# Graph attention on one core: digit products for two pairs at a time, and two PSUM banks for Q's products

## The chip, the cores and the metric

The kernel runs on one core of a Trainium2 chip. The metric is the device time of one execution in microseconds; lower is better.

## The reference

One layer of graph attention on 6,250 nodes with 512 features (8 heads of 64) and 106,250 edges, sorted by their target node `dst`, then two normalisations:

```python
Q, K, V = x @ Wq, x @ Wk, x @ Wv                    # each (6250, 8, 64)
score = einsum('ehd,ehd->eh', K[src], Q[dst]) / 8
score = exp(clip(score, -5, 5))
wV = segment_sum(V[src] * score[..., None], dst)    # (6250, 8, 64)
Z = segment_sum(score, dst)
h = x + wV / (Z + 1e-6)
h = (h - mean_over_nodes(h)) * rsqrt(var + 1e-5) * gamma + beta
out = layernorm(x + h)
```

## The kernel before

There are three stages, one behind the other. `project` computes Q, K and V by node and writes them to HBM, and builds the tables of the edges. `attend` walks over the edges. `normalise` does the rest. The change is in `attend` alone.

`attend` cuts the edges into visits of 128, each of which belongs to one tile of 128 target nodes. Two visits make a pair; there are 440 pairs. A ring has 8 places (`RING`), so the place `s` of pair `q` is `q % 8`. For a pair the engines do this:

- POOL gathers the 1024 K and V values of each edge's source node from HBM (L498), 6 pairs ahead of its own weighing.
- TensorE makes, from 7 binary digits of the target node within its tile, products that are equal to 7 where edge and node agree (`mm_ps`: L649 for the two visits by edge, L651 for both by node). These are called the digit products.
- ScalarE turns them into one-hot matrices by Relu with a bias of -7 (`mm_sb`, L582).
- TensorE multiplies the one-hots by the tile's Q, held as a high and a low part: four products of 512 columns, which bring Q's rows to the edges (`q_ps`, L640).
- VectorE multiplies them into K (L536), sums by head (L543) and clips (L546).
- ScalarE takes Exp (L585) and weighs 4 of V's 8 heads (L573, eight instructions a pair). VectorE weighs 2 heads (one pair later) and POOL 2 heads (six pairs later), both at L465.
- TensorE adds the weighed rows to their nodes in `acc` through the one-hots (L662). Where a tile ends, ScalarE copies it to `agg` (L567) and sets its bank to zero (L569): an eviction, 49 in all.

Each engine runs its own list of steps, one for each pair `q`, in an order written out by hand. Semaphores tie them together:

- ScalarE's step q: the Relu of pair q+3; then the wait for the clip, Exp and, in even steps, a DMA issue for the digits `lb`; the eight weighings of q; an eviction behind pair q-3, if one is due.
- TensorE's step q: Q's products of pair q+1; the digit products of q+3, which wait for the Relu of q+2 since there is one bank `mm_ps`; the products into `acc` for q-2.
- VectorE's step q: the multiply of q, the weighing of q-1, the reduction and the clip of q.

`q_ps` has three banks. A pair uses two of them, the middle one every time, in turn with the first and the last. The visit whose bank is free goes first; the other waits for VectorE's multiply of the pair before (`s_mul`).

Of the kernel before, what the change touches and what calls it, by code (L numbers as in the profile page):

```python
# [384 lines left out]
def attend(nc, kv_d, q_d, lb_d, nb_d, tabs, agg, soft):  # L385
    src_t, bits_row, cnt_row, ident = tabs
    with ExitStack() as ctx:
        def sb(name, shape, dt):
            return ctx.enter_context(nc.sbuf_tensor(name, shape, dt))
# [10 lines left out]
        kv = sb("kv", [P, RING, 2, KVW], F32)  # L400
        idx = sb("idx", [P, RING, 2], I32)
        q_tile = sb("q_tile", [P, 2, 2 * DIM], F32)
        mm_sb = sb("mm_sb", [P, RING, 4 * P], F32R)
        lb = sb("lb", [P, RING, 2 * P], BF16)
        nb = sb("nb", [P, P], BF16)
        raw = sb("raw", [P, RING, 2, HEADS], F32)
# [1 line left out]
        idle = sb("idle", [P, 1], F32)  # L408
        less = sb("less", [P, 1], F32)
        acc = ps("acc", [P, 2, 2 * DIM], F32)  # L410
        mm_ps = ps("mm_ps", [P, 4 * P], F32)
        q_ps = ps("q_ps", [P, 3, DIM], F32)


        s_g = [soft[f"s_g{s}"] for s in range(RING)]
        s_mul, s_red, s_clip, s_exp = sems("s_mul"), sems("s_red"), sems("s_clip"), sems("s_exp")
        s_t, s_mm, s_v, s_seg = sems("s_t"), sems("s_mm"), sems("s_v"), sems("s_seg")
        s_lb = [sem(f"s_lb{g}") for g in range(RING // LB_PAIRS)]
        s_idx = [sem(f"s_idx{g}") for g in range(RING // IDX_PAIRS)]
        s_nb, s_zero, s_qx, s_q, s_evc, s_evict = (sem("s_nb"), sem("s_zero"), sem("s_qx"), sem("s_q"),  # L420
# [20 lines left out]
        def follow(eng, tiles):  # L441
            now, before = eng.alloc_register("mask_now"), eng.alloc_register("mask_before")
            regs = [eng.alloc_register(f"tile_{n}") for n in range(tiles)]
            for r in (now, *regs):
                eng.reg_mov(r, 0)

            def fetch(mask):
                eng.reg_mov(before, now)
                if not isinstance(mask, int) or mask < MASKS:
                    eng.reg_load(now, bits_row[0:1, bass.ds(mask, 1)])  # L450

            def bit(k, earlier=False):
                mask = eng.snap(before if earlier else now, min_val=0, max_val=2 ** VBODY - 1)
                return (mask >> k) & 1
            fetch(0)
            return regs, fetch, bit

        def heads(ap):
            return ap.rearrange("p a (h d) -> p a h d", d=D_HEAD)
# [7 lines left out]
        with nc.Block() as block:  # L467
# [55 lines left out]
            @block.vector  # L523
            def _(dve):
                dve.memset(less[:, :], -float(BITS))
                dve.memset(lb[:, :, :], 0.0)
                dve.memset(nb[:, :], 0.0)
                dve.memset(zeros[:, :], 0.0).then_inc(s_zero, 1)

                def step(q, s, fills):  # L530
                    s1, f1 = at(s, fills, -1)
                    if there(q):
                        dve.wait_ge(s_g[s], 32 * fills)
                        dve.wait_ge(s_qx, q + 1)
                        k = kv[:, s, :, 0:DIM]
                        dve.tensor_tensor(k, q_ps[:, s % 2:s % 2 + 2, :], k,  # L536
                                          ALU.mult).then_inc(s_mul[s], 1)
                    if there(q - 1):
                        dve.wait_ge(s_exp[s1], f1)
                        weigh(dve, s1, ACT_HEADS, HEADS - ACT_HEADS - POOL_HEADS).then_inc(s_v[s1], 1)  # L540
                    if there(q):
                        dve.wait_ge(s_mul[s], fills)
                        dve.tensor_reduce(raw[:, s, :, :], heads(kv[:, s, :, 0:DIM]), AX.X,  # L543
                                          ALU.add).then_inc(s_red[s], 1)
                        dve.wait_ge(s_red[s], fills)
                        dve.tensor_scalar(raw[:, s, :, :], raw[:, s, :, :], -5.0, 5.0, ALU.max,  # L546
                                          ALU.min).then_inc(s_clip[s], 1)

                pipeline(dve, step)

            @block.scalar
            def _(act):
# [20 lines left out]
                    return act.activation(v, v, ACT.Copy, scale=kv[:, s, u, 2 * DIM + h:2 * DIM + h + 1])  # L573

                def step(q, s, fills):
                    e, a = q - LAG, q + 3
                    se, fe = at(s, fills, -LAG)
                    sa, fa = at(s, fills, 3)
                    if there(a):
                        act.wait_ge(s_t[sa], fa)  # L580
                        wait(act, s_seg[sa], fa - 1)
                        act.activation(mm_sb[:, sa, :], mm_ps[:, :], ACT.Relu, bias=less[:, 0:1]).then_inc(s_mm[sa], 1)  # L582
                    if there(q):
                        act.wait_ge(s_clip[s], fills)
                        act.activation(kv[:, s, :, 2 * DIM:KVW], raw[:, s, :, :], ACT.Exp).then_inc(s_exp[s], 1)  # L585
                        act.wait_ge(s_exp[s], fills)
                    if not isinstance(q, int) or q >= 0 and there(q + RING):
                        if s % LB_PAIRS == 0:
                            bits_of(q + RING, s)
                    if there(q):  # L590
                        for u in range(2):
                            for h in range(ACT_HEADS):
                                last = weighed(s, u, h)
                        last.then_inc(s_v[s], 1)
                    if there(e):
                        t0 = act.snap(tile_reg, min_val=0, max_val=TILES - 1)
                        over = act.snap(sum(bit((2 * (s - LAG) + n + VBODY - 2) % VBODY,
                                                earlier=2 * (s - LAG) + n + VBODY - 2 < VBODY) for n in (1, 2)),
                                        min_val=0, max_val=2)
                        with act.If(over > 0):  # L600
                            act.wait_ge(s_seg[se], fe)
                            evict(t0)
                            with act.If(over > 1):
                                evict((t0 + 1).with_bounds(min_val=1, max_val=TILES - 1))
                        act.reg_mov(tile_reg, t0 + over)
                    if s == RING - 1:
                        fetch(q // RING + 2 if isinstance(q, int) else fills + 1)
# [3 lines left out]
            def _(pe):  # L611
# [10 lines left out]
                def step(q, s, fills):  # L622
                    a, b, c = q + 3, q + 1, q - 2
                    (sa, fa), (sb_, fb), (sc, fc) = at(s, fills, 3), at(s, fills, 1), at(s, fills, -2)
                    if there(b):
                        tiles = []
                        for u in range(2):
                            v = 2 * sb_ + u
                            tile = pe.snap(pe.snap(tile_regs[(v - 1) % PLACES], min_val=0, max_val=TILES - 1)
                                           + bit(2 * s + u), min_val=0, max_val=TILES - 1)  # L630
                            pe.reg_mov(tile_regs[v % PLACES], tile)
                            tiles.append(tile)
                        pe.wait_ge(s_mm[sb_], fb)
                        pe.wait_ge(s_q, 16 * (tiles[1] + 1))
                        for u in ((0, 1), (1, 0))[sb_ % 2]:
                            if u == 1 - sb_ % 2:
                                wait(pe, s_mul[s], fills)
                            for n in range(2):
                                part_q = q_tile[:, bass.ds(tiles[u] % 2, 1), n * DIM:(n + 1) * DIM].bitcast(F32R)
                                last = pe.matmul(q_ps[:, sb_ % 2 + u, :], mm_sb[:, sb_, (2 + u) * P:(3 + u) * P],  # L640
                                                 part_q, start=(n == 0), stop=(n == 1))
                        last.then_inc(s_qx, 1)
                    if there(a):
                        if sa % LB_PAIRS == 0:
                            pe.wait_ge(s_lb[sa // LB_PAIRS], 16 * fa)
                        m1, f1 = at(s, fills, 2)
                        wait(pe, s_mm[m1], f1)
                        for u in range(2):
                            pe.matmul(mm_ps[:, u * P:(u + 1) * P], lb[:, sa, u * P:(u + 1) * P], nb[:, :],  # L649
                                      start=True, stop=True)  # L650
                        pe.matmul(mm_ps[:, 2 * P:4 * P], nb[:, :], lb[:, sa, :], start=True,  # L651
                                  stop=True).then_inc(s_t[sa], 1)
                    if there(c):
                        tiles = [pe.snap(tile_regs[(2 * sc + u) % PLACES], min_val=0, max_val=TILES - 1)
                                 for u in range(2)]
# [1 line left out]
                        pe.wait_ge(s_evict, tiles[1] + 1)  # L657
                        for u in range(2):
                            par = tiles[u] % 2
                            m = mm_sb[:, sc, u * P:(u + 1) * P].bitcast(F32)  # L660
                            for n in range(2):
                                last = pe.matmul(acc[:, bass.ds(par, 1), DIM - (1 - n) * HALF:DIM + n * HALF], m,  # L662
                                                 kv[:, sc, u, DIM + n * HALF:DIM + (n + 1) * HALF],
                                                 start=False, stop=True, skip_group_check=True)
# [299 lines left out]
```

## Time and profile before

| | |
|---|---|
| median of 3 runs | 2182.51 us (2182.19 to 2183.84) |
| the profiled execution | 2179.65 us, of which its span is 2177.7 |
| TensorE, VectorE, ScalarE, POOL busy | 95%, 74%, 66%, 62% of the span |
| edge stage, first to last multiply of VectorE | 530.4 to 1978.7 us |
| granted TensorE clock, mean | 0.989 of 2.4 GHz |

Times are microseconds from the span's start, unless they are marked ns. PE is TensorE's multiplication and PEld its weight load; DVE is VectorE, ACT ScalarE, POOL GpSimd. An idle time is put down to what ended it; "issue" is time in which the engine waited for nothing that the profile shows. Instructions of an engine overlap a little, so that sums of durations exceed busy time.

### The profile page before, as it was taken

The numbers are of one execution on the slowest core, as the hardware profiler recorded it, in microseconds if no ns is written. First come the engines' busy times: TensorE is split into PE (matmuls) and PEld (weight loads), VectorE is DVE, ScalarE is ACT, GpSimd is POOL, SyncE is SP. The second block draws the span as 40 slices with busy tenths as digits, with TensorE's granted clock in tenths as the row PEclk, the third lists the DMA queues.
The fourth block names the chain that finished last, engine by engine and source line by source line (L and its number), as shares of the span: only waits on it lengthen the run. The fifth ranks groups of instructions, "written<-read, shape, count | busy, mean of one in ns | idle before, by whom it ended". The sixth has DMA issues, their size and how long they took to land. (4 is left out here: it accounts for less than half of the span.)

```text
span 2177.7 us, 42941 instructions
## 1 busy us (share of the span) xinstructions
PE 2075.5 (95%) x8167; PEld 1328.3 (61%) x8168; DVE 1610.7 (74%) x2268; ACT 1429.6 (66%) x4869; POOL 1347.1 (62%) x1612
## 2 busy tenths in 40 slices
PE   8999999996999999999999999999999999998998
PEld 3444444443677677777777677777777777775343
DVE  3115311112899999999999999999899999998968
ACT  0001000101788888888888888888888888888745
POOL 2001444443788888888888888888888888882000
PEclk9999999998999999999999999999999999999999
DMA  5334665675799999899999899999899999996224
GB/s 182 132 120 155 229 220 214 224 238 214 269 322 325 319 328 321 313 321 323 318 331 325 311 318 325 318 332 323 308 322 323 317 329 330 312 315 217 89 97 174
DMA packets 184590, 588.14 MB, mean 270 GB/s; under 512 B 29072, under 2 KB 30832, under 8 KB 184560
## 3 DMA queue, kind: packets, MB, share of 16 engines
q0 software_dynamic: 135904, 465.14, 60.8%
q1 hardware_dynamic: 38080, 95.18, 12.5%
q10 hardware_dynamic: 10576, 27.50, 3.3%
q8 instruction: 9, 0.15, 0.0%
q14 instruction: 21, 0.17, 0.0%
HBM read 534.48 MB, written 78.91 MB: 282 GB/s over the span
## 5 line engine op out<-in xcount | busy, mean ns | idle before, releaser
L498 POOL DMA_INDIRECT kv<-kv_d,idx x880 | 905.1, 1029 | 236.1 <-issue 231.5
L573 ACT ACTIVATE kv<-kv 128x64 f32<-128x64 f32 x3520 | 889.2, 335 | 131.3 <-issue 76.5
L662 PE MATMUL acc<-kv,mm_sb 128*128 128x260 f32 x3520 | 875.8, 392 | 37.7 <-POOL kv L465 19.1
L662 PEld LDWEIGHTS acc<-kv,mm_sb 128*128 128x128 f32 x3520 | 635.4, 190 | 175.7 <-issue 96.2
L640 PE MATMUL q_ps<-q_tile,mm_sb 128*128 x1760 | 580.1, 445 | 23.1 <-issue 18.0
L536 DVE TENSOR_TENSOR kv<-q_ps,kv 128x1024 f32<-128x1024 f32 x440 | 538.4, 1224 | 48.5 <-PE q_ps L640 28.7
L543 DVE TENSOR_REDUCE raw<-kv 128x16 f32<-128x1024 f32 x440 | 532.3, 1210 | 0.0
L640 PEld LDWEIGHTS q_ps<-q_tile,mm_sb 128*128 128x128 f32 x1760 | 326.1, 189 | 130.1 <-issue 77.6
L270 ACT COPY kv_sb<-kv_ps 128x1024 f32<-128x1024 f32 x49 | 49.6, 1012 | 464.7 <-PE kv_ps L247 464.7
L247 PE MATMUL kv_ps<-w_sb,x_sb 128*128 128x512 f32 x784 | 344.5, 592 | 0.0
L582 ACT ACTIVATE mm_sb<-mm_ps,less 128x512 fp32r<-128x512 f32 x440 | 296.7, 674 | 68.0 <-PE mm_ps L651 41.7
L312 DVE TENSOR_SCALAR q_sb<-q_ps 128x512 fp32r<-128x512 f32 x49 | 33.9, 692 | 387.0 <-PE kv_ps L247 387.0
L465 POOL TENSOR_TENSOR kv<-kv 128x256 f32<-128x256 f32 x440 | 281.4, 640 | 17.5 <-ACT kv L585 9.3
L465 DVE TENSOR_TENSOR kv<-kv 128x256 f32<-128x256 f32 x440 | 235.2, 535 | 57.2 <-ACT kv L585 31.1
L247 PEld LDWEIGHTS kv_ps<-w_sb,x_sb 128*128 128x128 f32 x784 | 148.9, 190 | 187.5 <-issue 187.0
L247 PE MATMUL q_ps<-w_sb,x_sb 128*128 128x512 f32 x392 | 179.0, 599 | 6.9 <-DMA w_sb<-in_wq 6.9
L247 PEld LDWEIGHTS q_ps<-w_sb,x_sb 128*128 128x128 f32 x392 | 75.1, 192 | 101.3 <-issue 92.7
L649 PE MATMUL mm_ps<-nb,lb 128*128 128x128 bf16 x880 | 126.3, 225 | 5.4 <-ACT mm_sb L582 4.8
L546 DVE TENSOR_SCALAR raw<-raw 128x16 f32<-128x16 f32 x440 | 117.7, 267 | 15.2
L649 PEld LDWEIGHTS mm_ps<-nb,lb 128*128 128x128 bf16 x880 | 50.9, 98 | 125.7 <-issue 120.6
L651 PE MATMUL mm_ps<-lb,nb 128*128 128x256 bf16 x440 | 120.8, 275 | 0.0
L213 POOL DMA_DIRECT2D xb<-in_x x49 | 26.3, 536 | 131.4 <-DMA xb_d<-xb 128.6
(113 smaller groups left out, 971.4 us busy)
## 6 DMA issues: line engine op xcount, KB each, us to landing
kv_d<-kv_sb ACTq DMA_DIRECT2D x49, 512.0 KB, 4.4
q_d<-q_sb SPq DMA_DIRECT2D x49, 512.0 KB, 4.5
q_tile<-q_d SPq DMA_DIRECT2D x49, 512.0 KB
x_res<-xb_d SPq DMA_DIRECT2D x56, 256.0 KB, 5.3
kv<-kv_d,idx POOLq DMA_INDIRECT x880
x_sb<-in_xT SPq DMA_DIRECT2D x49, 256.0 KB, 2.7
xb<-in_x POOLq DMA_DIRECT2D x49, 256.0 KB, 3.0
xb_d<-xb POOLq DMA_DIRECT2D x49, 256.0 KB, 2.9
```

The lines of the kernel that those rows point to most:

```text
L247: last = pe.matmul(out, x_sb[j][:, c, :], w_sb[:, n, c, :], start=(c == 0), stop=(c == CHUNKS - 1))
L465: return eng.tensor_tensor(v, v, w, ALU.mult)
L498: pool.indirect_dma_start(kv[:, s, u, 0:2 * DIM], None, kv_d, bass.IndirectOffsetOnAxis(idx[:, s, u:u + 1], 0), bounds_check=N_NODES - 1, ...
L536: dve.tensor_tensor(k, q_ps[:, s % 2:s % 2 + 2, :], k, ALU.mult).then_inc(s_mul[s], 1)
L543: dve.tensor_reduce(raw[:, s, :, :], heads(kv[:, s, :, 0:DIM]), AX.X, ALU.add).then_inc(s_red[s], 1)
L546: dve.tensor_scalar(raw[:, s, :, :], raw[:, s, :, :], -5.0, 5.0, ALU.max, ALU.min).then_inc(s_clip[s], 1)
L573: return act.activation(v, v, ACT.Copy, scale=kv[:, s, u, 2 * DIM + h:2 * DIM + h + 1])
L582: act.activation(mm_sb[:, sa, :], mm_ps[:, :], ACT.Relu, bias=less[:, 0:1]).then_inc(s_mm[sa], 1)
L640: last = pe.matmul(q_ps[:, sb_ % 2 + u, :], mm_sb[:, sb_, (2 + u) * P:(3 + u) * P], part_q, start=(n == 0), stop=(n == 1))
L649: pe.matmul(mm_ps[:, u * P:(u + 1) * P], lb[:, sa, u * P:(u + 1) * P], nb[:, :], start=True, stop=True)
L651: pe.matmul(mm_ps[:, 2 * P:4 * P], nb[:, :], lb[:, sa, :], start=True, stop=True).then_inc(s_t[sa], 1)
L662: last = pe.matmul(acc[:, bass.ds(par, 1), DIM - (1 - n) * HALF:DIM + n * HALF], m, kv[:, sc, u, DIM + n * HALF:DIM + (n + 1) * HALF], sta ...
```

## The change

The digit products are made for two pairs at once, in TensorE's odd steps, into two banks (`mm_ps` by edge and by node): those of q+3 and q+4, behind the Relu of q+1 and q+2. One Relu of 1024 columns turns both banks into the one-hots of two pairs. It stands in ScalarE's even steps, is that of q+2 and q+3, and has moved from ahead of Exp to behind the eight weighings; the DMA issue for `lb` stands behind it. To make room, `q_ps` has two banks, and all four of Q's products wait for the multiply of the pair before. The semaphores `s_t` and `s_mm` count groups of two pairs. The core of the diff:

```diff
-        mm_sb = sb("mm_sb", [P, RING, 4 * P], F32R)
+        mm_sb = sb("mm_sb", [P, RING // 2, 2, 4 * P], F32R)
-        mm_ps = ps("mm_ps", [P, 4 * P], F32)
-        q_ps = ps("q_ps", [P, 3, DIM], F32)
+        mm_ps = ps("mm_ps", [P, 2, 4 * P], F32)
+        q_ps = ps("q_ps", [P, 2, DIM], F32)
+        def one_hot(s, u, by_node):
+            n = 2 * (s % 2) + u
+            return mm_sb[:, s // 2, by_node, n * P:(n + 1) * P]
...
-                        dve.tensor_tensor(k, q_ps[:, s % 2:s % 2 + 2, :], k,
+                        dve.tensor_tensor(k, q_ps[:, :, :], k,
...
-                    e, a = q - LAG, q + 3
+                    e, a = q - LAG, q + 2
-                    sa, fa = at(s, fills, 3)
-                    if there(a):
-                        act.wait_ge(s_t[sa], fa)
-                        wait(act, s_seg[sa], fa - 1)
-                        act.activation(mm_sb[:, sa, :], mm_ps[:, :], ACT.Relu, bias=less[:, 0:1]).then_inc(s_mm[sa], 1)
+                    sa, fa = at(s, fills, 2)
                     if there(q):
                         act.wait_ge(s_clip[s], fills)
                         act.activation(kv[:, s, :, 2 * DIM:KVW], raw[:, s, :, :], ACT.Exp).then_inc(s_exp[s], 1)
                         act.wait_ge(s_exp[s], fills)
-                    if not isinstance(q, int) or q >= 0 and there(q + RING):
-                        if s % LB_PAIRS == 0:
-                            bits_of(q + RING, s)
-                    if there(q):
                         for u in range(2):
                             for h in range(ACT_HEADS):
                                 last = weighed(s, u, h)
                         last.then_inc(s_v[s], 1)
+                    if s % 2 == 0 and there(a):
+                        act.wait_ge(s_t[sa // 2], fa)
+                        wait(act, s_seg[sa], fa - 1)
+                        wait(act, s_seg[sa + 1], fa - 1)
+                        act.activation(mm_sb[:, sa // 2, :, :], mm_ps[:, :, :], ACT.Relu,
+                                       bias=less[:, 0:1]).then_inc(s_mm[sa // 2], 1)
+                    if not isinstance(q, int) or q >= 0 and there(q + RING):
+                        if s % LB_PAIRS == 0:
+                            bits_of(q + RING, s)
...
-                        pe.wait_ge(s_mm[sb_], fb)
+                        pe.wait_ge(s_mm[sb_ // 2], fb)
                         pe.wait_ge(s_q, 16 * (tiles[1] + 1))
-                        for u in ((0, 1), (1, 0))[sb_ % 2]:
-                            if u == 1 - sb_ % 2:
-                                wait(pe, s_mul[s], fills)
+                        wait(pe, s_mul[s], fills if there(q) else 0)
+                        for u in range(2):
...
-                    if there(a):
-                        if sa % LB_PAIRS == 0:
-                            pe.wait_ge(s_lb[sa // LB_PAIRS], 16 * fa)
-                        m1, f1 = at(s, fills, 2)
-                        wait(pe, s_mm[m1], f1)
-                        for u in range(2):
-                            pe.matmul(mm_ps[:, u * P:(u + 1) * P], lb[:, sa, u * P:(u + 1) * P], nb[:, :],
-                                      start=True, stop=True)
-                        pe.matmul(mm_ps[:, 2 * P:4 * P], nb[:, :], lb[:, sa, :], start=True,
-                                  stop=True).then_inc(s_t[sa], 1)
+                    if s % 2 and there(a):
+                        pe.wait_ge(s_lb[sa // LB_PAIRS], 16 * fa)
+                        m1, f1 = at(s, fills, 1)
+                        wait(pe, s_mm[m1 // 2], f1)
+                        for n in range(4):
+                            pe.matmul(mm_ps[:, 0, n * P:(n + 1) * P], lb[:, sa + n // 2, n % 2 * P:(n % 2 + 1) * P],
+                                      nb[:, :], start=True, stop=True)
+                        pe.matmul(mm_ps[:, 1, :], nb[:, :], lb[:, sa:sa + 2, :], start=True,
+                                  stop=True).then_inc(s_t[sa // 2], 1)
```

## Rows read from the trace of the kernel before

**Rows 1.** The page, part 1: busy time of each engine.

```profile
PE 2075.5 (95%) x8167; PEld 1328.3 (61%) x8168; DVE 1610.7 (74%) x2268; ACT 1429.6 (66%) x4869; POOL 1347.1 (62%) x1612
```

**Rows 2.** One line's instructions: L536, min/median/max ns, first and last start.

```profile
L536 DVE TENSOR_TENSOR kv<-q_ps,kv x440: 1209/1225/1228, 530.4 to 1978.7; 128x1024 f32<-128x1024 f32 x147
```

**Rows 3.** Windows: PE, PEld, DVE, ACT, POOL busy; PEclk, DMA share, GB/s.

```profile
1000.00:1500.00 500.00, 481.92 (x2289) 356.10 (x2287) 464.23 (x612) 435.53 (x1562) 418.46 (x496) 1.00 0.91 322
```

**Rows 4.** Waits from 560 to 1990 us: total us, times, longest.

```profile
PEld mm_ps L649 <- issue: 117.9, 427, 2.7
DVE kv L536 <- PE q_ps L640: 18.2, 30, 1.6
```

**Rows 5.** Timeline, middle of the edge stage: start, us, then the instructions.

```profile
1191.92 1.22 DVE L536 TENSOR_TENSOR kv<-q_ps,kv 128x1024 f32<-128x1024 f32 x1
1192.25 2.02 PE L662 MATMUL acc<-kv,mm_sb 128*128 128x260 f32 x8
1193.45 2.02 ACT L573 ACTIVATE kv<-kv 128x64 f32<-128x64 f32 x8 [0.52 <-issue]
1193.91 1.28 PE L640 MATMUL q_ps<-q_tile,mm_sb 128*128 x4
1194.63 0.54 DVE L546 TENSOR_SCALAR raw<-raw 128x16 f32<-128x16 f32 x1
1195.04 0.28 PE L649 MATMUL mm_ps<-nb,lb 128*128 128x128 bf16 x2
1195.42 2.02 PE L662 MATMUL acc<-kv,mm_sb 128*128 128x260 f32 x8
1195.47 0.69 ACT L582 ACTIVATE mm_sb<-mm_ps,less 128x512 fp32r<-128x512 f32 x1
```

**Rows 6.** Timeline, end of the edge stage, where nothing is gathered.

```profile
1978.68 1.22 DVE L536 TENSOR_TENSOR kv<-q_ps,kv 128x1024 f32<-128x1024 f32 x1
1981.40 0.17 DVE L546 TENSOR_SCALAR raw<-raw 128x16 f32<-128x16 f32 x1
1981.61 0.21 ACT L585 ACTIVATE kv<-raw 128x16 f32<-128x16 f32 x1 [0.53 <-DVE raw L546]
1981.85 2.02 ACT L573 ACTIVATE kv<-kv 128x64 f32<-128x64 f32 x8
```

**Rows 7.** The page, part 5: busy us, mean ns, idle before.

```profile
L270 ACT COPY kv_sb<-kv_ps 128x1024 f32<-128x1024 f32 x49 | 49.6, 1012 | 464.7 <-PE kv_ps L247 464.7
L582 ACT ACTIVATE mm_sb<-mm_ps,less 128x512 fp32r<-128x512 f32 x440 | 296.7, 674 | 68.0 <-PE mm_ps L651 41.7
```

**Rows 8.** Timeline, ScalarE around an eviction.

```profile
1198.22 0.57 ACT L567 COPY agg<-acc  x1
1200.20 0.69 ACT L582 ACTIVATE mm_sb<-mm_ps,less 128x512 fp32r<-128x512 f32 x1 [0.73 <-issue]
```

**Rows 9.** Timeline, start of the edge stage: hand-overs between engines.

```profile
524.45 0.69 ACT L582 ACTIVATE mm_sb<-mm_ps,less 128x512 fp32r<-128x512 f32 x1 [3.49 <-PE mm_ps L651]
525.19 0.39 PE L649 MATMUL mm_ps<-nb,lb 128*128 128x128 bf16 x2 [0.78 <-ACT mm_sb L582]
...
555.17 1.28 PE L640 MATMUL q_ps<-q_tile,mm_sb 128*128 x4
556.56 1.23 DVE L536 TENSOR_TENSOR kv<-q_ps,kv 128x1024 f32<-128x1024 f32 x1 [1.60 <-PE q_ps L640]
```

**Rows 10.** Timeline, TensorE's waits and slow products near the stage's start.

```profile
528.25 2.07 PE L640 MATMUL q_ps<-q_tile,mm_sb 128*128 x4 [2.46 <-DMA q_tile<-q_d]
...
553.51 2.02 PE L662 MATMUL acc<-kv,mm_sb 128*128 128x260 f32 x8 [1.39 <-POOL kv L465]
...
571.94 0.37 PE L649 MATMUL mm_ps<-nb,lb 128*128 128x128 bf16 x2 [2.28 <-ACT mm_sb L582]
572.32 3.40 PE L662 MATMUL acc<-kv,mm_sb 128*128 128x260 f32 x8
```

**Rows 11.** Windows around those two waits, columns as in rows 3.

```profile
552.00:555.00 3.00, 1.61 (x9) 1.32 (x8) 2.93 (x5) 2.56 (x10) 2.52 (x4) 1.00 0.60 171
570.00:573.00 3.00, 1.06 (x5) 0.84 (x6) 1.07 (x2) 1.10 (x4) 2.58 (x4) 0.79 1.01 411
```

More of the change, by code:

```diff
@@ L410, in attend @@
         acc = ps("acc", [P, 2, 2 * DIM], F32)
-        mm_ps = ps("mm_ps", [P, 4 * P], F32)
-        q_ps = ps("q_ps", [P, 3, DIM], F32)
+        mm_ps = ps("mm_ps", [P, 2, 4 * P], F32)
+        q_ps = ps("q_ps", [P, 2, DIM], F32)
         s_g = [soft[f"s_g{s}"] for s in range(RING)]
         s_mul, s_red, s_clip, s_exp = sems("s_mul"), sems("s_red"), sems("s_clip"), sems("s_exp")
-        s_t, s_mm, s_v, s_seg = sems("s_t"), sems("s_mm"), sems("s_v"), sems("s_seg")
+        s_v, s_seg = sems("s_v"), sems("s_seg")
+        s_t, s_mm = ([sem(f"{name}{n}") for n in range(RING // 2)] for name in ("s_t", "s_mm"))
         s_lb = [sem(f"s_lb{g}") for g in range(RING // LB_PAIRS)]
@@ L632, in step @@
                             tiles.append(tile)
-                        pe.wait_ge(s_mm[sb_], fb)
+                        pe.wait_ge(s_mm[sb_ // 2], fb)
                         pe.wait_ge(s_q, 16 * (tiles[1] + 1))
-                        for u in ((0, 1), (1, 0))[sb_ % 2]:
-                            if u == 1 - sb_ % 2:
-                                wait(pe, s_mul[s], fills)
+                        wait(pe, s_mul[s], fills if there(q) else 0)
+                        for u in range(2):
                             for n in range(2):
                                 part_q = q_tile[:, bass.ds(tiles[u] % 2, 1), n * DIM:(n + 1) * DIM].bitcast(F32R)
-                                last = pe.matmul(q_ps[:, sb_ % 2 + u, :], mm_sb[:, sb_, (2 + u) * P:(3 + u) * P],
-                                                 part_q, start=(n == 0), stop=(n == 1))
+                                last = pe.matmul(q_ps[:, u, :], one_hot(sb_, u, 1), part_q, start=(n == 0),
+                                                 stop=(n == 1))
                         last.then_inc(s_qx, 1)
-                    if there(a):
-                        if sa % LB_PAIRS == 0:
-                            pe.wait_ge(s_lb[sa // LB_PAIRS], 16 * fa)
-                        m1, f1 = at(s, fills, 2)
-                        wait(pe, s_mm[m1], f1)
-                        for u in range(2):
-                            pe.matmul(mm_ps[:, u * P:(u + 1) * P], lb[:, sa, u * P:(u + 1) * P], nb[:, :],
-                                      start=True, stop=True)
-                        pe.matmul(mm_ps[:, 2 * P:4 * P], nb[:, :], lb[:, sa, :], start=True,
-                                  stop=True).then_inc(s_t[sa], 1)
+                    if s % 2 and there(a):
[7 more added lines that the diff above has]
+                                  stop=True).then_inc(s_t[sa // 2], 1)
                     if there(c):
@@ L659, in step @@
                             par = tiles[u] % 2
-                            m = mm_sb[:, sc, u * P:(u + 1) * P].bitcast(F32)
+                            m = one_hot(sc, u, 0).bitcast(F32)
                             for n in range(2):
```

## The prediction

> **What bounds the kernel now.** I read the page first, then the windows and the waits of the edge stage, then its timeline. The page shows TensorE busy for 95% of the span [rows 1]. That average covers three stages, and the change touches only the middle one. This stage's length is read from VectorE's multiply, which runs once a pair: 440 times, from 530.4 to 1978.7 us. That is 1448.3 / 439 = 3.30 us a pair, 1451.6 us for the 440 [rows 2]. In the middle of it TensorE is busy 96%, VectorE 93%, the DMA engines 91%, ScalarE 87% [rows 3]. So it is balanced, and small waits don't tell which engine leads. The waits of the stage are small: the multiply waits 18.2 us in all for Q's products [rows 4].
>
> The timeline gives TensorE's own round. The products into acc start at 1192.25 and again at 1195.42, so a round is 3.17 us: 1.66 from acc to Q's products, 1.13 from those to the digit products, 0.38 to the next acc [rows 5]. VectorE's round, from a multiply's start to the end of its clip, is 1195.17 - 1191.92 = 3.25 us there [rows 5] and 1981.57 - 1978.68 = 2.89 us where POOL gathers nothing [rows 6]. Both fit just under the 3.30 measured. No dependency longer than these is visible. The reason is in the code: ScalarE makes the one-hots of pair q+3 at the start of its step q, so they are ready two steps before TensorE needs them.
>
> **The change, part by part.**
>
> *The Relu moves and comes later.* This is the part that decides. After the change the Relu stands in ScalarE's even steps, behind the eight weighings, and makes the one-hots of q+2 and q+3. TensorE needs those of q+2 for Q's products in its step q+1, which come right behind the multiply of q+1. Nothing else is between. So a round of two pairs must pass through: clip of pair q, Exp, eight weighings, Relu, Q's products of q+2, multiply of q+2, reduction, clip of q+2. None of it can run ahead, since the Relu stands in ScalarE's order behind a wait for the clip of q. Its length, from rows:
>
> - clip's end to Exp: 1981.61 - 1981.57 = 0.04 [rows 6]
> - Exp to the first weighing: 1981.85 - 1981.61 = 0.24, taken as 0.25 [rows 6]. In even steps before, it took about 0.5 more with the DMA issue for lb between (0.52 at 1193.45 [rows 5]); that issue now stands behind the Relu.
> - the eight weighings: 2.02, and a Relu starts exactly at their end (1193.45 + 2.02 = 1195.47) [rows 5]
> - the Relu of 128x1024: not in the trace of before. A Relu of 128x512 takes 0.674 and a copy of 128x1024 takes 1.012 [rows 7]; a copy of 128x520 takes 0.57 [rows 8]. The slope is (1.012 - 0.57) / 504 = 0.88 ns an element, and 0.674 + 512 x 0.88 ns = 1.12. Bounds: 1.01 (the copy) and 1.35 (two Relus). I take 1.12, since the slope is that of the same engine reading the same memory.
> - the Relu's end to TensorE's first product: 525.19 - 525.14 = 0.05 [rows 9]
> - four Q products: 1.28 [rows 9]
> - their end to the multiply: 556.56 - 556.45 = 0.11 [rows 9]
> - multiply's start to the end of its clip, with the weighing of the pair before between: 2.89 to 3.25 as above; I take the middle, 3.07. VectorE's busy time says the same: 464.23 us for 612 instructions, four a pair, is 3.03 [rows 3].
>
> Sum: 0.04 + 0.25 + 2.02 + 1.12 + 0.05 + 1.28 + 0.11 + 3.07 = 7.94 us for two pairs, or 3.97 a pair against 3.30.
>
> *Does anything else in the two pairs take longer?* Put the multiply of pair 4 at 0. Its Q products started at -1.39, so the digit products start at -0.26 (1.13 behind). For two pairs they take at most twice 0.38, so acc(1) starts at 0.50 and the Q products of pair 5 at 2.16 (1.66 behind) [rows 5]. They wait for the multiply of pair 4, which is over at 1.22. They end at 3.44 and the multiply of pair 5 starts at 3.55; its clip ends at 6.62. acc(2) starts at 3.29 and ends at 5.31. Then TensorE stands at the Q products of pair 6 until the Relu ends: 3.07 + 0.04 + 0.25 + 2.02 + 1.12 = 6.50. The multiply of pair 6 starts at 6.55 + 1.28 + 0.11 = 7.94. VectorE has been free since 6.62, TensorE since 5.31. So TensorE's 6.3 us of work and VectorE's fit beside the chain. The weighing of pair 5 behind the multiply of pair 6 needs the Exp of pair 5, which ScalarE can start after the Relu and the clip of 5, at 6.66: in time.
>
> *Two banks for Q's products instead of three.* All four products of a pair now wait for the multiply of the pair before; half of them did already. Multiply 1.22 [rows 5], four products 1.28 and the two hand-overs of about 0.11 [rows 9] make 2.72 a pair. That is under the 3.17 of TensorE's round, and under half of 7.94. It costs nothing here: TensorE is in acc products when the multiply ends. Without that cover it would cost nothing still until the round is below 2.72.
>
> *Evictions, 49 of them.* From the copy's start to the next Relu 1.98 us pass on ScalarE [rows 8]. In an odd step an eviction starts behind the weighings of pair 5, which run from 6.95 to 8.97 here; ScalarE is free at about 10.95 and the Exp of pair 6 is due at 7.94 + 3.07 + 0.04 = 11.05. It fits with 0.1 to spare. In an even step it stands behind the Relu, 6.50, with the lb issue of up to 0.5 ahead, so ScalarE is free at about 9.0, which is when the weighing on VectorE wants the Exp of pair 5 (7.94 + 1.13). I add 0.1 an eviction, 5 us in all; if each cost its full 1.98 it would be 97 us, which nothing supports.
>
> *What is saved.* ScalarE's reading falls by 2 x 0.674 - 1.12 = 0.23 us for two pairs. TensorE's wait at issue before the digit products, 117.9 us over 427 times, 0.28 each [rows 4], comes once for two pairs. Both are off the new chain, except as counted: TensorE and ScalarE now have idle time. POOL and the gathers wait for acc of eight pairs back and have more time than before; the DMA share should fall to about 0.91 x 3.30 / 3.97 = 0.76. SP's loads of q_tile follow the Q products and are rare. The stages before and after are untouched.
>
> *Sum.* 220 x 7.94 = 1746.8, less 1451.6, is +295; with evictions +300. The profiled execution took 2179.65 us (span 2177.7 and 1.95 around it), so 2480; the median of the runs is 2.9 above the profiled one, so 2482.
>
> **The rivals.**
>
> *TensorE's clock falls as well.* In the forecast TensorE idles 6.55 - 5.31 = 1.24 us once in 7.94. The trace has a wait of 1.39 us with the granted clock at 1.00 all through, and one of 2.28 us behind which it was 0.79 and the next acc products were slow [rows 10, 11]. At the lower level four Q products took 2.07 instead of 1.28 [rows 10]. If that struck each round, +0.79 x 220 = +174 and the time is about 2656. For it: evictions lengthen single waits. Against it: 1.24 is on the side of the row that held. I give 9%. The Trainium skill (TensorE: Matmul & The Clock Gate, "A second HAM failure mode: psum-queue depth-cycling") tells of a kernel whose short idle times between groups of matmuls made the clock swing between its levels; by that rule this rival would be the likely one. The row with 1.39 us speaks against it, so far as one row can.
>
> *Faster.* The mechanism is one: the issue wait before the digit products is paid half as often, 220 x 0.28 = 62 us, on an engine whose round of 3.17 nearly sets the pace. That would give 2120. It decides only if the Relu's results are there when TensorE comes to them, that is if the chain through ScalarE is under TensorE's two rounds, 6.34. The chain's rows make 7.94, and even with each low bound 7.65. 3%.
>
> *No change.* The Relu is late only by what TensorE and VectorE have to do anyway, and the pace stays 3.3: this needs the chain to be under 6.6, so 1.3 us of its rows to be no part of it. 4%, at 2183.
>
> **How the numbers follow.** The forecast has 84%, the falling clock 9%, no change 4%, faster 3%. The chain with the copy's 1.01 for the Relu and 2.89 for VectorE is 7.65: 1683, that is 2414. With 1.35 and 3.25 it is 8.35: 1837, that is 2572, and an eviction cost of 40 us reaches 2610. I take 2400 to 2610, which holds the forecast's share and the mild part of the falling clock. A measurement here tells 0.2% (4 us) from nothing. Slower 0.93, same 0.04, faster 0.03.
>
> **What the profile of the changed kernel would show.** The multiplies 3.97 us apart on average, in turn about 3.6 and 4.4 (0 to 3.55, 3.55 to 7.94); before every second one VectorE idle for about 1.3 us, with Q's products named as the releaser. TensorE idle before Q's products of even pairs for some 1.2 us, with the Relu as releaser, 220 times. Relu 220 times at 1.12 us. ScalarE idle before Exp in even steps, with the clip as releaser. TensorE busy near 80%, DMA near 0.76, granted clock 0.98 or more. The prediction is wrong if the Relu's end is ahead of TensorE's arrival, if the chain starts from something other than the clip, or if the clock drops in the stage.

## The result: 2506 us, 15% slower

The changed kernel took 2506.49 us (median of 4 runs, 2503.65 to 2512.16) against 2182.74 before, a ratio of 1.149 (95% interval 1.1465 to 1.1506). The forecast was 2482, in a range of 2400 to 2610. The profiled execution took 2507.03 us with a span of 2505.3.

The page's busy times and two of its costliest groups (busy, mean ns, idle before):

```profile
PE 2124.8 (85%) x7947; PEld 1390.2 (55%) x7948; DVE 1599.7 (64%) x2268; ACT 1417.6 (57%) x4649; POOL 1355.6 (54%) x1612
...
L647 PE MATMUL q_ps<-q_tile,mm_sb 128*128 x1760 | 563.0, 443 | 334.9 <-ACT mm_sb L598 282.0
...
L598 ACT ACTIVATE mm_sb<-mm_ps,less 128x1024 fp32r<-128x1024 f32 x220 | 240.3, 1092 | 4.1 <-PE mm_ps L657 4.1
```

TensorE's busy share fell from 95% [rows 1] to 85%, while its busy time did not fall (2075.5 and 2124.8 us). The new idle time has a name: before Q's products, and the Relu ended it. The multiply's own line, and the windows of the middle of the stage (columns as in rows 3):

```profile
L543 DVE TENSOR_TENSOR kv<-q_ps,kv x440: 1210/1225/1226, 531.9 to 2305.7; 128x1024 f32<-128x1024 f32 x147
```

```profile
1000.00:1500.00 500.00, 404.70 (x1807) 306.68 (x1807) 375.34 (x497) 352.11 (x1213) 343.41 (x405) 0.96 0.79 262
```

1773.8 us lie between the first and the last multiply, 325.5 more than the 1448.3 of [rows 2]; that is the whole change. The pace is 4.04 us a pair, 8.08 for two. All engines are less busy than in [rows 3], so none of them is the bound. The waits from 560 to 2300 us (total, times, longest):

```profile
ACT kv L588 <- DVE raw L553: 500.9, 266, 3.4
...
DVE kv L543 <- PE q_ps L647: 334.0, 275, 3.0
PE q_ps L647 <- ACT mm_sb L598: 277.0, 172, 2.2
...
PE q_ps L647 <- DMA q_tile<-q_d: 38.8, 20, 2.7
```

The three large ones form a ring: ScalarE waits for VectorE, VectorE for TensorE, TensorE for ScalarE. In [rows 4] the wait of the multiply was 18.2. One round, from the timeline:

```profile
1205.02 0.22 ACT L588 ACTIVATE kv<-raw 128x16 f32<-128x16 f32 x1 [2.58 <-DVE raw L553]
1205.27 0.59 ACT L580 ACTIVATE kv<-kv 128x64 f32<-128x64 f32 x2
...
1207.19 1.09 ACT L598 ACTIVATE mm_sb<-mm_ps,less 128x1024 fp32r<-128x1024 f32 x1
...
1208.69 1.38 PE L647 MATMUL q_ps<-q_tile,mm_sb 128*128 x4 [2.02 <-ACT mm_sb L598]
...
1210.11 1.23 DVE L543 TENSOR_TENSOR kv<-q_ps,kv 128x1024 f32<-128x1024 f32 x1 [2.05 <-PE q_ps L647]
...
1210.75 3.00 PE L668 MATMUL acc<-kv,mm_sb 128*128 128x260 f32 x8
...
1212.83 0.17 DVE L553 TENSOR_SCALAR raw<-raw 128x16 f32<-128x16 f32 x1
1213.04 0.21 ACT L588 ACTIVATE kv<-raw 128x16 f32<-128x16 f32 x1 [2.60 <-DVE raw L553]
```

From Exp to Exp 8.02 us pass. Weighings, Relu, Q's products, multiply, clip and the next Exp follow each other with one gap that stands out: the Relu ends at 1208.28, and Q's products start 0.41 later. The acc products behind the 2.02 us wait are not in this round; they take 3.00 us where they took 2.02 in [rows 5]. From 1209.5 to 1212.9 the granted clock was 0.50, its lower level.

### The profile page after: what moved, and what is told of

Its sections match the earlier page's. It is cut to its first block and busy times, and to the rows that moved or that the text cites. A ratio compares the mean times of both kernels' runs of the same rounds, so it can differ in the third digit from the quotient of the medians.

```text
span 2505.3 us, 42557 instructions
## 1 busy us (share of the span) xinstructions
PE 2124.8 (85%) x7947; PEld 1390.2 (55%) x7948; DVE 1599.7 (64%) x2268; ACT 1417.6 (57%) x4649; POOL 1355.6 (54%) x1612
## 5 line engine op out<-in xcount | busy, mean ns | idle before, releaser
L505 POOL DMA_INDIRECT kv<-kv_d,idx x880 | 921.5, 1047 | 549.7 <-PE acc L668 348.5
L668 PE MATMUL acc<-kv,mm_sb 128*128 128x260 f32 x3520 | 895.5, 400 | 8.5 <-POOL kv L472 6.9
L647 PE MATMUL q_ps<-q_tile,mm_sb 128*128 x1760 | 563.0, 443 | 334.9 <-ACT mm_sb L598 282.0
L668 PEld LDWEIGHTS acc<-kv,mm_sb 128*128 128x128 f32 x3520 | 703.4, 201 | 140.8 <-issue 24.8
L588 ACT ACTIVATE kv<-raw 128x16 f32<-128x16 f32 x440 | 94.0, 214 | 522.4 <-DVE raw L553 510.8
L598 ACT ACTIVATE mm_sb<-mm_ps,less 128x1024 fp32r<-128x1024 f32 x220 | 240.3, 1092 | 4.1 <-PE mm_ps L657 4.1
L472 DVE TENSOR_TENSOR kv<-kv 128x256 f32<-128x256 f32 x440 | 208.7, 474 | 0.3 <-ACT kv L588 0.3
L655 PE MATMUL mm_ps<-nb,lb 128*128 128x128 bf16 x880 | 99.3, 242 | 0.8 <-DMA lb<-lb_d 0.8
L657 PE MATMUL mm_ps<-lb,nb 128*128 128x512 bf16 x220 | 96.5, 439 | 0.0
L655 PEld LDWEIGHTS mm_ps<-nb,lb 128*128 128x128 bf16 x880 | 57.2, 109 | 69.0 <-issue 68.0
```

Source lines behind the costliest of these rows:

```text
L472: return eng.tensor_tensor(v, v, w, ALU.mult)
L505: pool.indirect_dma_start(kv[:, s, u, 0:2 * DIM], None, kv_d, bass.IndirectOffsetOnAxis(idx[:, s, u:u + 1], 0), bounds_check=N_NODES - 1, ...
L598: act.activation(mm_sb[:, sa // 2, :, :], mm_ps[:, :, :], ACT.Relu, bias=less[:, 0:1]).then_inc(s_mm[sa // 2], 1)
L647: last = pe.matmul(q_ps[:, u, :], one_hot(sb_, u, 1), part_q, start=(n == 0), stop=(n == 1))
L655: pe.matmul(mm_ps[:, 0, n * P:(n + 1) * P], lb[:, sa + n // 2, n % 2 * P:(n % 2 + 1) * P], nb[:, :], start=True, stop=True)
L657: pe.matmul(mm_ps[:, 1, :], nb[:, :], lb[:, sa:sa + 2, :], start=True, stop=True).then_inc(s_t[sa // 2], 1)
```

## The experiments

Each ratio is to the kernel before in the same series of runs; differences of two experiments of different series are taken from ratios.

**The Relu first.**

```diff
                     sa, fa = at(s, fills, 2)
+                    if s % 2 == 0 and there(a):
+                        act.wait_ge(s_t[sa // 2], fa)
...
+                        act.activation(mm_sb[:, sa // 2, :, :], mm_ps[:, :, :], ACT.Relu,
+                                       bias=less[:, 0:1]).then_inc(s_mm[sa // 2], 1)
                     if there(q):
                         act.wait_ge(s_clip[s], fills)
...
```

> The changed kernel with its one Relu of 128x1024 moved to the start of ScalarE's even steps, ahead of Exp; everything else stays (two pairs at a time, two banks for Q's products). Theory: the loss comes from the round clip, Exp, weighings, Relu, Q's products, which this cuts. Then the pace is again near TensorE's round of 3.17 us a pair or a little under, since the issue wait before the digit products comes half as often: 2120 to 2190 us. Rival 1, the two banks of q_ps or the joint digit products cost the time: it stays near 2506. Rival 2, part of the loss is the lower clock by itself: it lands between, near 2300.

Measured: 2167.85 us, ratio 0.995 (0.9933 to 0.9966). The whole loss goes, with the joint digit products and the two banks still there, and the kernel is 0.5% faster than before. Rival 1 falls. Rival 2 falls in the form in which it was written, but this run can't price the clock, since its own mean clock is 0.991; the filler below does. Its waits from 600 to 1900 us show no wait for the Relu among the twelve largest, and the issue wait before the digit products, 106.4 us in 393 times in the same stretch of before, is halved:

```profile
PEld mm_ps L655 <- issue: 54.8, 200, 0.3
DVE kv L543 <- PE q_ps L647: 44.1, 62, 1.6
```

**The Relu late, but two pairs further ahead.**

```diff
-        LOOKAHEAD, LAG = 3, 3
+        LOOKAHEAD, LAG = 5, 3
...
-                    e, a = q - LAG, q + 2
+                    e, a = q - LAG, q + 4
...
-                    a, b, c = q + 3, q + 1, q - 2
...
+                    a, b, c = q + 5, q + 1, q - 2
...
-                        m1, f1 = at(s, fills, 1)
+                        m1, f1 = at(s, fills, 3)
```

> The changed kernel with the Relu left behind the weighings, but made for pairs q+4 and q+5 instead of q+2 and q+3 (digit products for q+5 and q+6 in TensorE's odd steps, engines start two steps earlier). Theory: the round through ScalarE then closes over four pairs instead of two, 7.94 us plus at most two of TensorE's pairs of 3.17 beside it, and no longer binds: 2120 to 2200 us. Rival, the place of the Relu in ScalarE's order is what costs (it delays the next Exp): near 2506, or at least above 2350.

Measured: 2210.59 us, ratio 1.0147 (1.013 to 1.0164). The rival falls: the place behind the weighings is not what costs 324 us, the short lead is. The time is 11 us over what I expected, and the waits from 600 to 1900 us show a likely reason, a wait that the kernel before has 3 times for 0.7 us:

```profile
PE mm_ps L655 <- ACT mm_sb L598: 48.2, 114, 1.1
```

TensorE's digit products need the one set of mm_ps banks back, so they still wait for a late Relu. I had not counted that wait.

**The Relu in the middle**, behind four of the eight weighings.

```diff
                             for h in range(ACT_HEADS):
                                 last = weighed(s, u, h)
+                            if u == 0:
+                                relu()
...
```

`relu()` holds the Relu with its waits, unchanged.

> The changed kernel with the Relu behind the first four of the eight weighings. Theory: the round of two pairs loses 1.01 us: about 8.08 - 1.01 = 7.07 us, 3.53 a pair, 220 x 1.01 = 222 us less than 2506, that is 2285, a little more if other waits fill in (2270 to 2330). Rival, the round is not what sets the pace: no change by more than 50 us, or straight back to 2180.

Measured: 2295.77 us, ratio 1.0537 (1.0519 to 1.0554). Half of the weighings' 2.02 us off the round gives 211 us (207 by the ratios) of the 222 worked out. The granted clock from 700 to 1900 us is 1.00 here, so the 116 us that are left over the kernel before are lost at the full clock.

**The Relu directly behind Exp.** The diff is the one above with `relu()` ahead of the loop.

> The changed kernel with the Relu directly behind Exp, ahead of the eight weighings. Theory: the round loses all 2.02 us of weighings: 8.08 - 2.02 = 6.06 us for two pairs, which is under TensorE's two rounds of 6.3, so the pace is set elsewhere and the time is 2165 to 2205 us. Rival, a straight line from the changed kernel through the Relu behind four weighings (2296) would give 2296 - 211 = 2085.

Measured: 2180.42 us, ratio 0.9983 (0.9972 to 0.9993). So the first 1.01 us off the round brings 207 us by the ratios and the second 121. The mean round with the Relu in the middle was 7.10 us in the trace; 1.01 less is 6.09, under the 6.60 us that two pairs take in the kernel before. So the round has stopped being the bound on the way.

**Two banks in the kernel before.**

```diff
-        q_ps = ps("q_ps", [P, 3, DIM], F32)
+        q_ps = ps("q_ps", [P, 2, DIM], F32)
...
-                        for u in ((0, 1), (1, 0))[sb_ % 2]:
-                            if u == 1 - sb_ % 2:
-                                wait(pe, s_mul[s], fills)
+                        wait(pe, s_mul[s], fills if there(q) else 0)
+                        for u in range(2):
```

> The kernel before with two banks for Q's products instead of three, and all four waiting for the multiply of the pair before; nothing else changed. Theory: TensorE comes to Q's products when the multiply has ended, so it costs nothing: 2175 to 2200 us. Rival, the lost bank is part of the change's loss: 30 to 100 us more than before, 2210 to 2280.

Measured: 2186.83 us, ratio 1.0032 (1.002 to 1.0045). Not quite nothing: 7 us, the cost of the lost bank with its wait. In the waits from 600 to 1900 us a row has grown from the 0.3 us in 2 times of before:

```profile
PE q_ps L639 <- DVE kv L536: 11.5, 21, 0.8
```

**The Relu split in two**, one of 128x512 for each bank, at its late place.

```diff
-                        act.activation(mm_sb[:, sa // 2, :, :], mm_ps[:, :, :], ACT.Relu,
-                                       bias=less[:, 0:1]).then_inc(s_mm[sa // 2], 1)
+                        for n in range(2):
+                            last = act.activation(mm_sb[:, sa // 2, n, :], mm_ps[:, n, :], ACT.Relu,
+                                                  bias=less[:, 0:1])
+                        last.then_inc(s_mm[sa // 2], 1)
```

> The changed kernel with its Relu of 128x1024 split into two of 128x512, one for each bank, at the same place. Theory: they take 2 x 0.67 = 1.34 us less about 0.1 of overlap instead of 1.09, and the round of two pairs grows by 0.15 to 0.25 us, all of it on the chain: 220 x 0.15 to 0.25 = +33 to +55 us, 2540 to 2562. Rival, the Relu is not on the chain: 2506, no change.

Measured: 2547.6 us (2533.12 to 2557.65), ratio 1.1682 (1.1649 to 1.1715): 41 us more than the changed kernel, 43 by the ratios, as a longer link of the round should cost. In the trace the two take 1.24 us together instead of 1.09, which is 32 us over 220 rounds. The profiled execution was the fastest of the four (2533.12). What adds the rest is not shown.

**The kernel before with a late Relu**: its Relu of q+3 moved behind the weighings.

> The kernel before (one pair at a time, three banks, Relu of pair q+3) with the Relu moved behind the eight weighings of step q. Theory: it closes a round over three pairs: 0.04 + 0.25 + 2.02 + 0.67 + 0.05 to TensorE's digit products, 0.38 + 1.66 to Q's products of q+3, 1.28 + 0.11 + 3.07 to the next clip, 9.5 us in three pairs or 3.18 a pair, just under the 3.30 measured: 2180 to 2240 us. Rival, the place behind the weighings costs by itself, whatever the lead: 2400 or more.

Measured: 2246.5 us, ratio 1.0284 (1.0265 to 1.0304), 6 us over the upper end that I expected. With a lead of three pairs the same place costs 62 us instead of 324. TensorE waits for the Relu at its digit products here (56.0 us in 134 times from 600 to 1900 us), as in the run with the longer lead. The pace is 3.46 us a pair where the worked-out round gave 3.18; what makes up the difference was not taken apart.

**A filler for TensorE.** It keeps TensorE busy for part of its wait for the Relu.

```diff
+FILL = 3
...
+                        wait(pe, s_mul[s], fills if there(q) else 0)
+                        if s % 2 and there(q):
+                            for n in range(FILL):
+                                pe.matmul(q_ps[:, 1, 0:P], ident[:, :], ident[:, :], start=True, stop=True)
                         pe.wait_ge(s_mm[sb_ // 2], fb)
                         pe.wait_ge(s_q, 16 * (tiles[1] + 1))
-                        wait(pe, s_mul[s], fills if there(q) else 0)
```

> The changed kernel with three float32 products of the 128x128 identity in TensorE's odd steps, into a bank of q_ps that the next Q products overwrite, so that TensorE works while it waits for the Relu. They compute nothing that is used. In the changed kernel the granted clock of the edge stage is 0.94 to 0.96. Theory: the clock falls in single waits only and is a small part of the loss; with the clock back at 0.99 or more the time falls by 5 to 30 us: 2475 to 2502. Rival, the falling clock is a main part of the loss: below 2450. If the filler runs over the Relu's end it costs up to its overrun, 0.1 to 0.3 us a round, 20 to 60 us more.

Measured: 2477.93 us, ratio 1.1351 (1.1329 to 1.1372). The windows show the clock back at its upper level:

```profile
1000.00:1500.00 500.00, 428.62 (x2211) 349.21 (x2210) 380.61 (x507) 355.41 (x1225) 346.96 (x411) 1.00 0.80 266
```

The gain is 29 us, but not all of it is the clock's. The mean gap from the Relu's end to Q's products was 0.30 us here and 0.42 in the changed kernel. Two more runs take that apart.

**The order of TensorE's waits.** In the source, one run takes the multiply's wait first, the other has the order multiply, q_tile, Relu.

> The changed kernel with TensorE's wait for the multiply taken first and those for the Relu and for q_tile behind it, the order that the filler run had, but without the filler. Mean hand-over from the Relu's end to Q's first product: 0.42 us in the changed kernel, 0.31 with the filler. Theory: that came from the order of the waits, so it is 0.31 here too, and 0.11 x 220 = 24 us are saved: 2478 to 2488, with the granted clock still near 0.95. Rival, the filler's gain was the clock's: 2500 to 2510 here.

Measured: 2504.64 us, ratio 1.148 (1.1464 to 1.1497), with the gap at 0.42. The time is the rival's, but the rival is not proved by it: the edit did not change the order in which the waits ran (below).

> The changed kernel with TensorE's waits in the order multiply, q_tile, Relu: the one that ends last stands last. Theory: what is left behind it is the work on registers for the address of q_tile; the hand-over falls to 0.15 to 0.25 us and the time to 2455 to 2475. Rival, the waits are free and the hand-over is all address work: as with the order before it, no gain beyond 5 us.

Measured: 2485.29 us, ratio 1.1396 (1.1378 to 1.1415), mean granted clock 0.961, gap 0.31. It is over the range I expected, yet a gain beyond the rival's 5 us: 20 us by the ratios.

The trace records which semaphore each of TensorE's instructions waits for. Behind the Relu's end it has, in every round between 700 and 1900 us (mean start behind the Relu's end, us):

| run | Relu's wait | multiply's wait | register instruction with q_tile's wait | first weight load |
|---|---|---|---|---|
| changed kernel | 0.04 | 0.14 | 0.26 | 0.41 |
| multiply's wait first in the source | 0.04 | 0.14 | 0.26 | 0.41 |
| Relu's wait last in the source | 0.04 | ahead of the Relu's | 0.15 | 0.30 |
| filler | 0.04 | at the filler's first weight load | 0.14 | 0.30 |

So the waits do not run in the order of the source. In the run with the multiply's wait first it still ran behind the Relu's, as in the changed kernel, and that is why nothing changed. In the run with the Relu's wait last, q_tile's still ran behind it; only the multiply's had moved ahead. With the filler it had moved to the filler itself, and that is where its shorter gap comes from. One wait behind the Relu's, for something long done, costs 0.11 us a round: 0.11 x 220 = 24 us, and 20 were measured. With the gaps nearly equal (0.31 and 0.30), the run with the Relu's wait last and the filler differ by the filler and the clock: 1.1396 - 1.1351 = 0.45%, about 10 us.

**The early Relu, split in two.**

> The kernel with the Relu at the start of ScalarE's even steps (2168 us, 0.995 of before) with its Relu split into two of 128x512. Theory: ScalarE has slack there and the gain is that of the joint digit products on TensorE, so it stays within 5 us of 2168. Rival, the gain came from ScalarE's shorter Relu: 2180 or more.

Measured: 2175.33 us, ratio 0.9965 (0.9952 to 0.9977), against 0.995 (0.9933 to 0.9966) unsplit. The time is 7 us over the 2168 that was named, so just outside the 5 us expected; by the ratios it is 3 us. The intervals overlap. By the ratios most of the gain stays without the fused Relu; how much of the rest is the Relu's own can't be told.

## Why the prediction was right, and where a term was off

The deciding step held: a round of two pairs through clip, Exp, weighings, Relu, Q's products and multiply. Removing the Relu's dependence on the clip, lengthening the lead, and shortening or lengthening the round each moved the time as that round says.

The terms against their means in the changed kernel, over 148 rounds between 700 and 1900 us of its timeline, in us:

| term | forecast | measured |
|---|---|---|
| clip's end to Exp | 0.04 | 0.03 |
| Exp to weighings | 0.25 | 0.25 |
| weighings, to the Relu's start | 2.02 | 1.93 |
| Relu 128x1024 | 1.12 | 1.09 |
| Relu's end to Q's products | 0.05 | 0.42 |
| four Q products | 1.28 | 1.25 |
| to the multiply | 0.11 | 0.04 |
| multiply's start to the clip's end | 3.07 | 3.05 |
| sum | 7.94 | 8.05 |

One term was mis-sized, "the Relu's end to TensorE's first product: 0.05". It came from a digit product whose weight load itself waits for the Relu [rows 9]. The kernel before with a late Relu has 52 such hand-overs, at 0.05, and 181 in which a second wait, for `lb`, takes part, at 0.11. Q's products have two more waits behind the Relu's and an operand at an address out of a register; the trace has a register instruction at each of them (min/median/max ns):

```profile
L647 PEldq FUSED_REGOPS  x1760: 51/74/115, 529.5 to 2304.8; - x196
```

Of the 0.42, 0.11 is the multiply's satisfied wait, as the runs above show, and about 0.15 lies between the register instruction with q_tile's wait and the first weight load. How much of that is the wait and how much the address was not taken apart. The other terms were 0.25 too long together, most of it in overlaps that I added twice: the Relu starts before the last weighing ends, and the multiply was taken 0.11 behind the products instead of 0.04. So the sum is nearer than its terms, in part by luck. The error left is 0.11 us a round by the table and 0.14 by the pace of the whole stage (8.08), 25 to 31 us, less the 5 us for evictions that were not there: that is the miss, 2506 against 2482.

Smaller steps:

- Evictions, "5 us in all": 33 rounds with one took 8.06 us from Relu to Relu, 115 without took 8.05. They cost at most 0.01 us each.
- "It costs nothing here", of the two banks: that held in the changed kernel as far as the trace shows (0.3 us of waits of Q's products for the multiply), but not for the order of the waits: the multiply's wait, though satisfied, ran behind the Relu's and cost the 0.11 us above. In the kernel before the same edit costs 7 us, so the claim that it would cost nothing without that cover was wrong.
- The falling clock, a rival with 9%: it came in part. The prediction named it as a sign of being wrong ("if the clock drops in the stage") and forecast 0.98 or more; the mean of the execution was 0.956 and that of 700 to 1900 us 0.95. TensorE idled longer than the forecast 1.24 us (324 us in 215 rounds is 1.5, with single waits of 2.02 and more), partly because of the gap of 0.42. Yet only 19 of 148 rounds had Q's products over 1.35 us. It was worth about 10 us, not 174. The trace has 33 stretches of 3.4 us at the lower level between 700 and 1900 us, and of these 113 us at most 35 fell on the Q products that stand in the round. The Trainium skill (TensorE: Matmul & The Clock Gate, "A second HAM failure mode: psum-queue depth-cycling") tells of short idle times between groups of matmuls that make the clock swing; the trace agrees that the clock swings, and the filler shows that it mattered little here.
- The faster rival's condition is met with the Relu first. It gave 12 us, not 62. The issue waits before the digit products fell by 51.6 us from 600 to 1900 us, but those before acc's weight loads rose by 30.8 (87.9 to 118.7). TensorE and VectorE are now about as busy as each other (columns as in [rows 3], where VectorE has 464.23); which of them sets the pace is not shown:

```profile
1000.00:1500.00 500.00, 476.12 (x2187) 357.39 (x2224) 472.31 (x615) 430.98 (x1494) 421.10 (x500) 1.00 0.91 323
```

- The 20 waits put down to q_tile, 38.8 us, are waits for the Relu too: in each of the 20, Q's products start 0.41 to 0.44 us behind a Relu's end, as behind the waits that the trace puts down to the Relu.
- The picture of the pairs came out: the multiplies are 3.49 and 4.58 us apart in turn (forecast 3.6 and 4.4), and VectorE idles 1.49 us before every second one (1.3).
- Small slips of the working: the weighings of pair 5 start at 6.91, not 6.95, and the lower end of the range leaves out the 5 us for evictions that the upper end holds. Neither changes a result.

## What to carry to other kernels

Where engines run hand-ordered steps with leads, follow every dependency until it returns to the same engine, and divide its length by the number of steps that it spans. That round is a bound of its own, though every engine has idle time. Work that depends on nothing in its step belongs ahead of the first wait of the step: here one moved Relu turned a ratio of 1.149 into 0.995. When a round runs over a hand-over, price it from a hand-over with the same kind of operand and as many waits, and keep waits that are long satisfied from running behind the one that ends last. Read their order from the trace: here it was not the order of the source, and a run that changed only the source's order measured nothing.

## What the runs showed of the hardware

- From a Relu's end to a product with a register address, 0.42 us passed with the multiply's and q_tile's waits behind the Relu's, and 0.31 with q_tile's alone. To a digit product at a fixed address it was 0.05 where the weight load itself waited for the Relu [rows 9], and 0.11 with one more wait (181 times in the kernel before with a late Relu).
- A Relu of 128x1024 with a bias operand, out of two PSUM banks, took 1.09 us; one of 128x512 0.67.
- In the changed kernel TensorE idled 1.48 us before Q's products in each round of 8.05 us, at most 2.14, and the granted clock from 700 to 1900 us was 0.95. With the filler it idled 1.12 us, at most 1.46, and in the 7.1 us rounds of the middle position 0.92, at most 1.30; in both the clock there was 1.00.
